# Attention scores of a Flamingo layer: 32-row matmuls on four row strips in place of full matmuls on a block-diagonal copy of k

## The reference

```python
q = rms_norm(linear(layernorm(x), q_w, q_b), norm_q_w)       # 16 heads of 32
k = rms_norm(linear(context, k_img_w, k_img_b), norm_k_img_w)
v = linear(context, v_img_w, v_img_b)
probs = softmax(einsum('bqhd,bkhd->bhqk', q, k) / sqrt(32))
x = x + tanh(g_xattn) * linear(einsum('bhqk,bkhd->bqhd', probs, v), o_w, o_b)
x = x + tanh(g_ffn) * ffn(layernorm(x))                      # relu^2 MLP 512-2048-512, plus a routed expert term
```

## Time and profile before

| what | value |
|---|---|
| three runs | 1548.4, 1550.09, 1550.29 us |
| median | 1550.09 us |
| span of the profiled execution | 1548.3 us |
| TensorE busy in the span | 1499.5 us (97%) |
| VectorE, ScalarE, GpSimd busy | 892.5, 689.9, 443.8 us |
| mean granted TensorE clock | 0.992 |

### The profile page before, as it was taken

One profiled execution on the slowest core, in us unless ns is written; L12 is line 12 of the kernel. 1 busy time (PEld: TensorE's weight loads), 2 busy tenths in 40 slices (PEclk: granted clock), 3 DMA queues, 4 the chain that ended last, 5 costly groups with the idle time before them and its releaser, 6 DMA issues.

```text
span 1548.3 us, 22150 instructions
## 1 busy us (share of the span) xinstructions
PE 1499.5 (97%) x6912; PEld 1201.4 (78%) x6912; DVE 892.5 (58%) x1474; ACT 689.9 (45%) x1951; POOL 443.8 (29%) x582
## 2 busy tenths in 40 slices
PE   5999999999999999989999999999999999999996
PEld 4777777777777777767878878878788788788785
DVE  6877777777777777774634334353353343433524
ACT  5667677766676777664422222222222222222221
POOL 3455545444555454440002011020020120200202
PEclk9999999999999999999999999999999999999998
DMA  7222222222222222414310010010100100210100
GB/s 232 62 83 79 68 76 81 70 73 81 81 75 67 81 81 68 123 42 136 109 55 28 1 62 20 14 61 7 54 27 0 54 27 1 67 41 0 41 14 27
DMA packets 76353, 91.75 MB, mean 59 GB/s; under 512 B 7072, under 2 KB 39968, under 8 KB 76320
## 3 DMA queue, kind: packets, MB, share of 16 engines
q1 hardware_dynamic: 76320, 91.34, 19.3%
HBM read 57.76 MB, written 16.78 MB: 48 GB/s over the span
## 4 chain that ended last, share of the span: by engine, by line
PE 78%; DVE 10%; ACT 6%; issue 3%; POOL 1%; DMA 1%; SPq 1%; ACTq 0%; DVEq 0%; POOLq 0%
PE bank L73 14%; PE bank L75 14%; PE bank L74 14%; PE wide L73 10%; PE wide L74 10%; PE wide L75 10%; DVE kf L455 3%; PE bank L270 3%; DVE pT_lo L374 2%; DVE qf L479 2%; ACT pT_hi L537 2%; ACT junk_q L602 1%; ACT junk_k L585 1%; PE bank L824 1%; PE bank L290 1%
## 5 line engine op out<-in xcount | busy, mean ns | idle before, releaser
L1082 ACT ACTIVATE relu<-bank 128x512 f32<-128x512 f32 x128 | 76.7, 599 | 423.6 <-PE bank L75 423.6
L1120 DVE TENSOR_TENSOR hid<-relu 128x512 f32<-128x512 f32 x128 | 97.1, 759 | 269.5 <-ACT relu L1082 269.4
L558 ACT ACTIVATE prob<-wide,nmx 128x128 f32<-128x128 f32 x512 | 180.6, 403 | 39.3 <-DVE nmx L401 39.3
L73 PE MATMUL wide<-down_hi,hT_hi 128*128 128x512 f32 x384 | 152.2, 396 | 0.0
L75 PE MATMUL bank<-wk_hi,up_lo 128*128 128x512 f32 x384 | 152.0, 396 | 0.0
L74 PE MATMUL wide<-down_lo,hT_hi 128*128 128x512 f32 x384 | 151.6, 395 | 0.0
L74 PE MATMUL bank<-wk_lo,up_hi 128*128 128x512 f32 x384 | 151.6, 395 | 0.0
L73 PE MATMUL bank<-wk_hi,up_hi 128*128 128x512 f32 x384 | 151.6, 395 | 0.0
L75 PE MATMUL wide<-down_hi,hT_lo 128*128 128x512 f32 x384 | 151.5, 394 | 0.0
L1122 DVE TENSOR_TENSOR hT_lo<-hid,hT_hi 128x512 fp32r<-128x512 f32 x128 | 89.6, 700 | 89.8 <-ACT hT_hi L1071 89.8
L670 POOL TENSOR_TENSOR prob<-prob,rr 128x512 f32<-128x512 f32 x128 | 137.8, 1087 | 0.0
(11 more groups left out here) (156 smaller groups left out, 3624.7 us busy)
## 6 DMA issues: line engine op xcount, KB each, us to landing
kd<-kT SPq DMA_DIRECT2D x128, 128.0 KB, 2.4
xin<-in_x SPq DMA_DIRECT2D x32, 256.0 KB, 2.7
cin<-in_ctxT SPq DMA_DIRECT2D x32, 256.0 KB, 2.6
xres<-in_x SPq DMA_DIRECT2D x32, 256.0 KB, 2.7
x_scratch<-x SPq DMA_DIRECT2D x32, 256.0 KB, 2.0
fx<-x_scratch SPq DMA_DIRECT2D x32, 256.0 KB, 2.7
fres<-x_scratch SPq DMA_DIRECT2D x32, 256.0 KB, 4.0
out_x<-fres SPq DMA_DIRECT2D x32, 256.0 KB, 2.0
```

What stands on the lines that cost most here:

```text
L73: eng.matmul(dst, ah, bh, start=first and k == 0, stop=False)
L558: i = act.activation(prob[:, g, h * P:(h + 1) * P], cols(bank[g], h), ACT.Exp, bias=nmx[:, n:n + 1], scale=1.0, accum_out=rs[:, n:n + 1])
L1082: act.activation(ff.relu[:, :], bank[4 + i % 2], ACT.Relu).then_inc(ff.ac_r, 1)
L1120: dve.tensor_tensor(ff.hid[:, :], ff.relu[:, :], ff.relu[:, :], ALU.mult).then_inc(ff.dv_h, 1)
```

## The change

The copy `kd`, its memsets, its DMAs and their semaphores go. The features of q and k are laid out anew: the columns of the weights wq and wk, of their biases and of the norm row are taken in the order (s g d) in place of (g s d), so that after the transpose tile s holds, in strip g (partitions 32g to 32g + 31), head 4g + s. Scores are then matmuls of 32 rows: weights are a strip of q (32 x 128), the moving operand is the same strip of `kT` (32 x 128 columns), and four matmuls in a row go to four strips and four banks. There are 4 x 3 x 4 = 48 a slot. `pe_S` is raised once, after the last.

```diff
-            kd = sb(ctx, "kd", [P, 2, NG, HG, P], F32R)
...
+            def by_strip(a):
+                return a.rearrange("p (g s d) -> p s g d", g=NG, s=HG)
+            def as_strips(a):
+                return a.rearrange("p (s g d) -> p s g d", g=NG, s=HG)
+            def staged(n, k):
+                return by_strip(w_stage[n][:, k, :]) if n < 2 else w_stage[n][:, k, :]
+            def part(n, i, k):
+                a = W[WN[n]][i][:, k, :]
+                return as_strips(a) if n < 2 else a
...
-                    row(nqk, "nq", ld_n)
+                    row(qf, "nq", ld_n)
...
-                        if first(b):
-                            sp.wait_ge(kdz, 2)
-                        at_least(sp, ac_kT, b + 1, apart=True)
-                        at_least(sp, dv_kT, b + 1, apart=True)
-                        for h in range(HG):
-                            sp.dma_start(kd[strip(h), :, :, h, :].bitcast(F32), kT[strip(h), :, :, :].bitcast(F32)).then_inc(kd_in, DMA)
...
                 def scores(b):
                     at_least(pe, dv_qT, b + 1)
-                    at_least(pe, kd_in, (b + 1) * (HG * DMA))
-                    for g in range(NG):
-                        mm3(pe, bank[g], [(cols(qT_hi, g), cols(qT_lo, g))],
-                            [tuple(kd[:, n, g, :, :].rearrange("p h k -> p (h k)") for n in range(2))]).then_inc(pe_S, 1)
+                    at_least(pe, dv_kT, b + 1)
+                    for h in range(HG):
+                        for n, (q, m) in enumerate(((qT_hi, 0), (qT_hi, 1), (qT_lo, 0))):
+                            for g in range(NG):
+                                mm = pe.matmul(cols(bank[g], h), cols(q, h)[strip(g), :], kT[strip(g), m, h, :],
+                                               start=n == 0, stop=n == 2)
+                    mm.then_inc(pe_S, 1)
...
-                    at_least(dve, pe_S, b * NG + (g + 1))
+                    at_least(dve, pe_S, b + 1)
...
-                    sub(lo[:, k, :], w_stage[n][:, k, :], hi[:, k, :]).then_inc(wl, 1)
+                    sub(part(n, 1, k), staged(n, k), part(n, 0, k)).then_inc(wl, 1)
...
-                    dve.memset(kd[:, 0, :, :, :].bitcast(mybir.dt.uint32), 0).then_inc(kdz, 1)
...
-                        dve.tensor_tensor(kb[:, :], BK, bk[:, :], ALU.add).then_inc(dv_kb, 1)
+                        dve.tensor_tensor(as_strips(kb[:, :]), as_strips(BK), by_strip(bk[:, :]), ALU.add).then_inc(dv_kb, 1)
...
-                            dve.tensor_tensor(nqk[:, :], nqk[:, :], junk_q[:, :], ALU.mult).then_inc(cst, 1)
+                            dve.tensor_tensor(as_strips(nqk[:, :]), by_strip(qf[:, :]), by_strip(junk_q[:, :]), ALU.mult).then_inc(cst, 1)
...
-                        dve.tensor_tensor(qb[:, :], BQ, bq[:, :], ALU.add).then_inc(dv_qb, 1)
+                        dve.tensor_tensor(as_strips(qb[:, :]), as_strips(BQ), by_strip(bq[:, :]), ALU.add).then_inc(dv_qb, 1)
...
-                    copy(W[WN[n]][0][:, k, :], w_stage[n][:, k, :]).then_inc(wh, 1)
+                    copy(part(n, 0, k), staged(n, k)).then_inc(wh, 1)
...
-                        at_least(act, kd_in, b * (HG * DMA))
+                        at_least(act, pe_S, b)
...
-                    pool.memset(kd[:, 1, :, :, :].bitcast(mybir.dt.uint32), 0).then_inc(kdz, 1)
```

More of the change, by code:

```diff
@@ L134, in flamingo_layer @@
             ld_x, ld_c, ld_r = ([sem(f"{s}{n}") for n in range(2)] for s in ("ld_x", "ld_c", "ld_r"))
-            wh, wl, cst, kdz, kd_in = sem("weights_hi"), sem("weights_lo"), sem("row_consts"), sem("kd_zero"), sem("kd_in")
+            wh, wl, cst = sem("weights_hi"), sem("weights_lo"), sem("row_consts")
             pe_K, pe_Q, pe_Tx, pe_TP, pe_PV, pe_Tk, pe_Tq, pe_S, pe_O = (
@@ L411, in weight_lo @@
                 def weight_lo(n, k):
-                    hi, lo = W[WN[n]]
                     dve.wait_ge(wh, n * KT + k + 1)
-                    sub(lo[:, k, :], w_stage[n][:, k, :], hi[:, k, :]).then_inc(wl, 1)
+                    sub(part(n, 1, k), staged(n, k), part(n, 0, k)).then_inc(wl, 1)
                 def before():
-                    dve.memset(kd[:, 0, :, :, :].bitcast(mybir.dt.uint32), 0).then_inc(kdz, 1)
                     stats(0, 0)
```

## The result

The changed kernel takes **1560.1 us** (median of 4 runs, 1559.9 to 1561.2) against 1550.2 for the kernel before; the ratio is 1.0064, with a 95% interval of 1.0049 to 1.0078. It is slower, as forecast, but by 10 us and not by 109. The measured time lies in the range that was given, but 99 us from its likeliest value, and no case of the prediction ended there: rival 1 had 1534, the next case 1575. That it lies inside is luck, since the range was drawn from one case to the other.

What follows compares the result with a forecast made beforehand. It took a slot as a ring of waits through all engines, 20.85 us each; (5.23 - 1.75) x 31 = +107.9, slot 0 +2.5, a copy stall of 1.0 gone: +109, so 1659 us, range 1532 to 1672.

Steps and rivals of the forecast that it cites:

- rival 1: TensorE's score pairs: four strips load and compute side by side, S = 1.30 us, 1534 us in all; chance 24%.
- the next case: TensorE's score pairs: loads overlap in part, 54 ns a pair, S = 2.6 us, 1575 us in all; chance 26%.
- The new scores: TensorE: S, the length of a slot's 48 score matmuls with loads one after another, 0.109 us a pair, is 5.23 us.
- Lost overlap: VectorE's first maximum waits for all scores, starting S - 0.98 us later; each slot changes by S - 1.75 us.
- this balance: Length of TensorE's scores at which a slot neither gains nor loses: S = 1.75 us, 36 ns for each new matmul.
- The ring: Chain of waits round a slot, 20.85 us; the delay was to pass from maxima over exponentials to pT_hi, junk_k, kf.
- 0.77 us to spare: Slack by which the exponentials' end lay under TensorE's work ahead of pT_hi of group 0, in the kernel before.
- kb now has ScalarE's extra 1 us as cover: VectorE's kb add: a slower bias read would be hidden; without cover +22 us for one add.
- Taken at nothing: Edits counted as zero: DMAs leaving the SP queue, memsets, moved waits, bias adds at 0.68 us, kf and qf collisions.
- the term for rival 1: Slot 0's first maximum under rival 1: starts at 29.0 us, behind the vb add, -1.4 us.
- the signs named beforehand: Profile after: scores' starts within 5.1 to 5.4 us, maximum 0.2 later, pT_hi behind exponentials, slots 24.3; overlapping loads would refute.
- Direction: Whole kernel: slower 70%, same 7%, faster 23%.

Runs made afterwards that it cites:

- the run strip by strip: Changed kernel with the loop over the strips outermost, so 12 matmuls in a row go to one strip before the next; 1657.7 us, ratio 1.0689.
- the last row of the table: Kernel before, with v_hi and v_lo moved into the slot after, v_lo ahead of the multiplication of group 3; 1558.3 us, ratio 1.0047.
- the same new order: v_hi and v_lo moved into the slot after, v_lo ahead of the multiplication of group 3: 1532.0 us on the changed kernel, 1558.3 on the kernel before.
- 1/std first: Changed kernel with 1/std of the batch after next ahead of the multiplication of group 0 in GpSimd's list; 1550.5 us, ratio 0.9999.
- v_lo beside it: Changed kernel with 1/std first and v_lo on GpSimd behind the multiplication of group 1; 1554.1 us, ratio 1.0024.
- v_lo ahead of the multiplication of group 3: Changed kernel with v_hi and v_lo moved into the slot after, v_lo before the multiplication of group 3 on GpSimd; 1532.0 us, ratio 0.9874.

## Why the prediction was wrong

*The new scores.* This is the step that failed: "I take 0.109 a pair: S = 48 x 0.109 = 5.23 us". A pair on one strip does cost that, 0.112 in the run strip by strip, but four go at once: S = 12 x 0.112 = 1.34 and 0.15 at the ends, 1.49 by the trace. The row of 16 rows and 8 columns was the nearest in shape and the wrong one in kind, since its neighbours in the stream are on the same strip; it could say what a load costs and nothing of whether loads of different strips wait for each other. No row of before could. The first rival had it right (S = 1.30), and the rule of the Trainium skill ("TensorE: Matmul & The Clock Gate", Part 3) is borne out: starts 3 to 4 ns apart, and 48 pairs in 1.49 us that take 4.34 strip by strip.

*Lost overlap.* "Each slot changes by S - 1.75 us" named the right mechanism, one signal after the last score, but the wrong branch behind it. With S = 1.49 it gives -0.26 a slot, a kernel faster by 8 us; rival 1, with this balance, had 1534, and it too was wrong by 26. The branch that it followed came out nearly as it said: pT_hi of group 0 was to start at S + 7.22 = 8.71 and starts at 8.57. But junk_k, which it put straight behind, starts at 9.81, since it waits for kb. The ring does not close over the end of the exponentials and pT_hi but over v_hi, v_lo, multiplication 0, rstd, xn and kb: junk_k is 8.09 us behind the first maximum. With the 0.22 between S and the maximum, the balance is 9.47 - 8.09 - 0.22 = 1.16 us, 24 ns a pair, and 1.49 - 1.16 = +0.33 a slot, against 0.35 measured. S = 1.49 is 31 ns a pair, above it. The fork in the kernel before had not one branch with 0.77 us to spare but another with 0.2: kb at 8.55 ends at 9.23, and junk_k starts at 9.47. What kb stands behind was in the timeline of before:

```profile
307.87 1.25 DVE L387 TENSOR_SCALAR xn<-xin,mv,rstd 128x512 f32<-128x512 f32 x1 [0.36 <-POOL rstd L648]
309.05 0.68 DVE L434 TENSOR_TENSOR kb<-bank,bk 128x512 f32<-128x512 f32 x1
```

xn waits for rstd, and kb starts as xn ends (309.12), in the same moment in which the k projection lets it (8.54 in the last row of the table, where xn is long done). The prediction read kb's start as the lag behind the k projection alone, and passed over the rest with "kb now has ScalarE's extra 1 us as cover", a cover worked out for kb's adding of the bias, not for kb starting late.

*Taken at nothing.* The adds of q and k take 678 ns with their new patterns, as before. kf and qf are 1440 and 1419 ns as ever. In slot 0 the maxima start at 28.8, 1.6 us earlier than before, as the term for rival 1 had it (29.0). The copy cost 1.4 us; 1.0 was said. Of the signs named beforehand, the first maximum 0.2 us behind the scores and pT_hi of group 0 straight behind the last exponential came; the score matmuls of a slot starting within 5.1 to 5.4 us (it is 1.29) and slots of 24.3 us (21.2) did not, and loads of different strips overlap in the records, which was named as the sign of a wrong forecast.

*Direction.* Slower was right by luck: with the right S the prediction's own balance gives a faster kernel. By the step that failed and the one that was half right the errors were 31 x 3.74 = +116 and, for the balance, 31 x 0.6 = -18 us, together the 98 or 99 us of the miss.

What stays open: whether maxima could start before all scores are done at full overlap. In this kernel each strip has a bank of its own, and each bank is complete only at the end. Taking maxima of the finished columns while TensorE writes others of the same bank was not tried. The Trainium skill, "PSUM — Partial Sum Buffer", section on bank collisions, says that two engines must not touch one bank and quadrant at a time, even in other columns; no run here shows it.

## What to carry to other kernels

Where an edit moves the first member of a ring, follow every list that is behind it, engine by engine, up to where they meet again, and write down the slack of each; the smallest decides, and a branch of tiny instructions on GpSimd can be it. A shorter matmul phase is worth only what its consumers can start earlier: pay for four strips at once with one late signal, and the order behind it has to be made anew; with that done the same scores gave 1532 us, where the kernel before has 1550 and, in the same new order, 1558.

## What the runs showed of the hardware that was not expected

Four 32-row matmuls on four strips, each with its own 128-column float32r load, take 112 ns together; two strips take 111 to 112, and one strip as much for a single one. At a border between strips the stream runs at 57 ns a pair for some seven matmuls.

In the run strip by strip, with TensorE's records showing no idle time, the granted clock fell to its lower level once a slot, 3.8 to 5.4 us after the first score matmul, in 23 of slots 3 to 27, and was back some 3 us later (in one slot 7); the median stretch behind the scores is 1.5 us longer. With two or four strips at a time the clock stayed at its upper level in all of these slots.

VectorE's times change with GpSimd's order: xn takes 0.70 us with 1/std first and 1.43 with v_lo beside it, kf 1.44 in most runs and 1.78 with v_lo ahead of the multiplication of group 3.
